# Attention values divided in their transposed layout after small transfers, and the context tiles transposed beside the value tiles

## The reference, cut to what matters

```python
# x: (8, 512, 256); ctx: (8, 1601, 256); 16 heads of 16; 704 hidden
def attention(query, ctx):                       # per batch
    q, k, v = split_heads(query @ Wq.T + bq), split_heads(ctx @ Wk.T + bk), split_heads(ctx @ Wv.T + bv)
    attn = softmax(einsum('bhqd,bhkd->bhqk', q, k) / 4)
    out = einsum('bhqk,bhkd->bhqd', attn, v)     # merged heads: (512, 256)
    return out @ Wo.T + bo
x = x + attention(layernorm(x), ctx)
h = layernorm(x)                                 # fp4_linear rounds both operands
h = silu(fp4_linear(h, w_gate)) * fp4_linear(h, w_up)
x = x + fp4_linear(h, w_down)                    # to a 4-bit grid in blocks of 16
```

## Time and profile before

| | before |
|---|---|
| median of 3 runs | 1804.52 us (1801.16 to 1804.56) |
| the profiled execution: time, span | 1801.16 us, 1799.4 us |
| mean granted clock of TensorE | 0.984 |
| TensorE busy | 1687.2 us (94%) |
| VectorE busy | 1398.6 us (78%) |
| ScalarE busy | 1155.4 us (64%) |
| GpSimd busy | 528.4 us (29%) |
| loop iteration | about 210 us |

### The profile page before, as it was taken

The page is one execution under the profiler, slowest core; times in us unless marked ns, Lnnn a source line. Parts: engine busy times, 40 slices in busy tenths (PEclk is TensorE's granted clock), DMA queues, the critical chain, the costliest instruction groups (busy, mean ns, idle before and its releaser), DMA issues.

```text
span 1799.4 us, 26659 instructions
## 1 busy us (share of the span) xinstructions
PE 1687.2 (94%) x9600; PEld 658.4 (37%) x9600; DVE 1398.6 (78%) x1969; ACT 1155.4 (64%) x2335; POOL 528.4 (29%) x409
## 2 busy tenths in 40 slices
PE   3799789999999999999999999999999999989978
PEld 2332124333343343433443333433334334423425
DVE  6777887888868887788878888688877887688538
ACT  2366567776667666776667766676667766666651
POOL 4316340442107320152204421073201622012213
PEclk8899999999999999999999999999999999999989
DMA  6643432142323322043221423243220422300000
GB/s 147 151 77 92 90 77 37 47 116 38 55 37 96 91 49 50 13 110 73 55 52 44 118 40 55 37 96 90 50 48 12 108 40 43 52 1 1 7 18 12
DMA packets 98031, 109.09 MB, mean 61 GB/s; under 512 B 18788, under 2 KB 83308, under 8 KB 97900
## 3 DMA queue, kind: packets, MB, share of 16 engines
q1 hardware_dynamic: 93344, 103.26, 27.1%
q10 hardware_dynamic: 4556, 4.13, 1.1%
HBM read 76.78 MB, written 30.16 MB: 59 GB/s over the span
## 4 chain that ended last, share of the span: by engine, by line
PE 74%; DVE 15%; ACT 7%; issue 3%; DMA 1%; ACTq 0%; POOL 0%; SPq 0%; DVEq 0%; POOLq 0%
PE pvb L714 19%; PE st L685 18%; PE mx L699 9%; PE misc L632 7%; DVE cmx L941 6%; PE misc L582 5%; ACT prob L870 4%; PE misc L589 4%; PE misc L644 2%; PE misc L652 2%; PE misc L521 1%; PE misc L640 1%; PE misc L611 1%; PE misc L570 1%; PE misc L559 1%
## 5 line engine op out<-in xcount | busy, mean ns | idle before, releaser
L870 ACT ACTIVATE prob<-st 128x512 f32<-128x512 f32 x1630 | 887.6, 599 | 419.9 <-PE st L685 418.2
L941 DVE TENSOR_REDUCE cmx<-mx 128x2 f32<-128x1024 f32 x768 | 905.3, 1219 | 215.4 <-PE mx L699 211.7
L685 PE MATMUL st<-qstack,kstack 112*128 112x512 bf16 x1630 | 520.6, 386 | 32.6 <-ACT prob L870 20.0
L714 PE MATMUL pvb<-prob,vv 128*17 128x512 f32 (+1 forms) x3328 | 440.7, 601 | 0.6 <-ACT prob L870 0.6
L685 PEld LDWEIGHTS st<-qstack,kstack 112*128 112x128 bf16 x1630 | 128.4, 98 | 554.9 <-issue 315.7
L699 PE MATMUL mx<-kstack,qstack 48*128 48x512 bf16 (+1 forms) x2048 | 253.3, 336 | 32.8 <-DMA qstack<-scr_q 16.3
L1202 POOL TENSOR_TENSOR cin<-cin 128x400 f32<-128x400 f32 (+1 forms) x60 | 55.3, 922 | 418.6 <-ACT cin L798 418.6
L1235 POOL TENSOR_TENSOR ht<-ht,rh 128x704 f32<-128x704 f32 x29 | 40.2, 1385 | 425.0 <-DVE rh L917 425.0
L632 PE MATMUL misc<-wguT,rowsT 128*128 128x352 f32 x456 | 154.9, 462 | 0.0
L699 PEld LDWEIGHTS mx<-kstack,qstack 48*128 48x128 bf16 x2048 | 58.0, 94 | 195.7 <-issue 147.2
L632 PEld LDWEIGHTS misc<-wguT,rowsT 128*128 128x128 f32 x456 | 87.1, 191 | 41.4 <-issue 1.0
(11 more groups left out here) (201 smaller groups left out, 1593.3 us busy)
## 6 DMA issues: line engine op xcount, KB each, us to landing
kstack<-scr_k SPq DMA_DIRECT2D x384, 100.1 KB, 4.3
scr_k<-cin SPq DMA_DIRECT2D x48, 300.0 KB, 3.2
qstack<-scr_q SPq DMA_DIRECT2D x372, 32.0 KB, 1.9
cin<-ctx_in SPq DMA_DIRECT2D x8, 1280.0 KB, 6.6
scr_q<-qp SPq DMA_DIRECT2D x15, 384.0 KB, 5.4
scr_k<-cin SPq DMA_DIRECT2D x16, 300.8 KB, 4.4
xn<-x SPq DMA_DIRECT2D x8, 512.0 KB, 3.9
x<-x SPq DMA_DIRECT2D x8, 512.0 KB, 3.8
```

The lines of the kernel that those rows point to most:

```text
L685: mm(score_bank(it, n, pair, h)[0:KROWS[kt], :], kstack[:, hd, KOFF[kt]:KOFF[kt] + KROWS[kt]], qstack[:, hd, :], start=True, stop=True).th ...
L714: last = mm(pvb[32 * h:32 * h + D + 1, :], vv[0:w, kt, HG * g + h, :], prob[0:w, n % 2, h, :], start=(kt == 0), stop=(kt == NKT - 1))
L870: activate(prob[0:KROWS[kt], n % 2, 2 * pair + h, :], score_bank(it, n, pair, h)[0:KROWS[kt], :], ACT.Exp, scale=SCALE).then_inc(exp_done[ ...
L941: v.tensor_reduce(cmx[:, g % 2, h0:h0 + 2, at:at + 1], products, op=ALU.max, axis=AX.X).then_inc(max_free, 1)
```

## The change

- `vv` holds, for each pair of heads, 16 values, 16 ones, 16 values. A head's weights are 32 columns (values and ones, or ones and values), so `pvb` has for each head 16 rows of weighted values and 16 rows that all hold the sum of weights.
- `pvT`, `attT`, `den`, `attTr` and `group_divided` go. After the copy to `pvs`, SP moves for each group four pieces of 16 rows by 512 to `att`, whose layout is now the transposed one, and four to `sums` (`values_in`; in the tail ScalarE's queue takes the four of `sums`). When two groups are there, VectorE takes the reciprocal of `sums` in place (512 columns) and multiplies `att` in place (`values_divided`), in steps 37 and 3. `o` reads `att`.
- Context tiles are transposed one by one, as a `guest` of the value tile of the same number: the two transposes go into the free half of its bank, behind its matmuls. ScalarE copies them behind the values. `ctx2`, two tiles at once, is left for the start.
- `q` 0, `q` 1 and the keys stand in other steps, and GpSimd's work follows: in step 16 `xround` now comes first, then the split of `k` 4.
- `nm` 1 is in step 9; `bias` waits for value tile 9; `xnT` shares its memory with `mt`, so `xpower` waits for `q` 1.
- SP's order: the values' transfers come in, and the keys of one half are stored together.

```diff
 SLOTS = {
-    0: ([("v", 8, "att")], [("ctxT", 0, "early")]),
-    1: ([("v", 9, "att")], [("pvT", 3, "late")]),
-    2: ([("v", 10, "att")], [("attT", 0, "late")]),
-    3: ([("v", 11, "att")], [("attT", 1, "late")]),
-    4: ([("v", 12, "att")], [("ctxT", 1, "early")]),
-    5: ([("o", 0, "late")], [("ctxT", 2, "early")]),
-    6: ([("o", 1, "late")], [("ctxT", 3, "early")]),
-    7: ([("ctxT", 4, "early")], [("ctxT", 5, "early")]),
-    8: ([("ctxT", 6, "early")], [("xnT", 0, "early")]),
-    9: ([("k", 0, "early")], [("xnT", 1, "early")]),
-    10: ([("k", 1, "early")], [("nm", 1, "att")]),
-    11: ([("k", 2, "early")], []),
-    12: ([("q", 0, "early")], []),
+    0: ([("v", 8, "att")], [("ctx2", 0, "once")]),
+    1: ([("v", 9, "att")], [("ctx2", 1, "once")]),
+    2: ([("v", 10, "att")], [("ctx2", 2, "once")]),
+    3: ([("v", 11, "att")], [("ctx2", 3, "once")]),
+    4: ([("v", 12, "att")], []),
+    5: ([("o", 0, "late")], []),
+    6: ([("o", 1, "late")], []),
+    7: ([("xnT", 0, "early")], []),
+    8: ([("xnT", 1, "early")], []),
+    9: ([("q", 0, "early")], [("nm", 1, "att")]),
+    10: ([("k", 0, "early")], []),
+    11: ([("k", 1, "early")], []),
+    12: ([("k", 2, "early")], []),
     13: ([("k", 3, "early")], []),
-    14: ([("k", 4, "early")], []),
-    15: ([("q", 1, "early")], []),
+    14: ([("q", 1, "early")], []),
+    15: ([("k", 4, "early")], []),
     16: ([("k", 5, "early")], []),
     17: ([("k", 6, "early")], []),
-    18: ([("pvT", 0, "att")], [("xqT", 0, "late")]),
-    19: ([("k", 7, "early")], [("xqT", 1, "late")]),
+    18: ([("xqT", 0, "late")], [("xqT", 1, "late")]),
+    19: ([("k", 7, "early")], []),
...
-    31: ([("gate", 5, "late")], [("pvT", 1, "att")]),
+    31: ([("gate", 5, "late")], []),
...
-    41: ([("down", 2, "late")], [("pvT", 2, "att")]),
+    41: ([("down", 2, "late")], []),
...
 DVE_EXTRA = {
-    1: [("late", "norm", 3)], 5: [("late", "stats", 0)], 6: [("late", "stats", 1)], 7: [("late", "mean", 0)], 8: [("late", "root", 0)],
-    9: [("late", "apply", 0)], 10: [("att", "nm", 1)], 11: [("late", "apply", 1)], 12: [("late", "xmax", 0)], 13: [("late", "xscale", 0)],
-    14: [("late", "xmul", 0)], 15: [("late", "xpower", 0)], 17: [("late", "xlast", 0)], 19: [("att", "norm", 0)],
+    3: [("late", "values", 1)], 5: [("late", "stats", 0)], 6: [("late", "stats", 1)], 7: [("late", "mean", 0)], 8: [("late", "root", 0)],
+    9: [("att", "nm", 1)], 10: [("late", "apply", 0)], 11: [("late", "apply", 1)], 12: [("late", "xmax", 0)], 13: [("late", "xscale", 0)],
+    14: [("late", "xmul", 0)], 15: [("late", "xpower", 0)], 17: [("late", "xlast", 0)],
...
-    31: [("att", "norm", 1)], 33: [("late", "hscale", 2)], 34: [("late", "hpower", 2)], 35: [("att", "nm", 3)], 39: [("late", "hscale", 3)], 40: [("late", "hpower", 3)],
-    42: [("att", "norm", 2)], 43: [("next", "stats", 0)], 44: [("next", "stats", 1)], 45: [("next", "mean", 0)], 46: [("next", "root", 0)],
+    33: [("late", "hscale", 2)], 34: [("late", "hpower", 2)], 35: [("att", "nm", 3)], 37: [("att", "values", 0)], 39: [("late", "hscale", 3)], 40: [("late", "hpower", 3)],
+    43: [("next", "stats", 0)], 44: [("next", "stats", 1)], 45: [("next", "mean", 0)], 46: [("next", "root", 0)],
...
 POOL_WORK = {
-    0: [("late", "bias", 0)], 10: [("early", "k", 0)], 11: [("early", "k", 1)], 12: [("early", "k", 2)], 13: [("early", "q", 0)],
-    14: [("early", "k", 3)], 15: [("early", "k", 4)], 16: [("early", "q", 1), ("late", "xround", 0)], 17: [("early", "k", 5)], 18: [("early", "k", 6)], 20: [("early", "k", 7)],
+    0: [("late", "bias", 0)], 10: [("early", "q", 0)], 11: [("early", "k", 0)], 12: [("early", "k", 1)], 13: [("early", "k", 2)],
+    14: [("early", "k", 3)], 15: [("early", "q", 1)], 16: [("late", "xround", 0), ("early", "k", 4)], 17: [("early", "k", 5)], 18: [("early", "k", 6)], 20: [("early", "k", 7)],
...
+            def values_in(it, g, part):
+
+                sp.wait_ge(pvs_done, it.count(part, NG, g + 1))
...
+                for h in range(HG):
+                    row = HALF * s + D * h
+                    values, weights = 2 * D * h + D * (h % 2), 2 * D * h + D * (1 - h % 2)
+                    sp.dma_start(att[row:row + D, c, :], pvs[values:values + D, :]).then_inc(values_row[g], 16)
+                    if it.kind != "tail":
+                        sp.dma_start(sums[row:row + D, :], pvs[weights:weights + D, :]).then_inc(values_row[g], 16)
...
                     last.then_inc(full[kind], 1)
+                    if guest(it, job):
+                        context_tile(guest(it, job))
...
-                        last = mm(pvb[32 * h:32 * h + D + 1, :], vv[0:w, kt, HG * g + h, :], prob[0:w, n % 2, h, :], start=(kt == 0), stop=(kt == NKT - 1))
+                        last = mm(pvb[2 * D * h:2 * D * (h + 1), :], vv[0:w, kt, (HG * g + h) // 2, D * (h % 2):D * (h % 2 + 2)], prob[0:w, n % 2, h, :], start=(kt == 0), stop=(kt == NKT - 1))
...
+                def values_divided(part, c):
+
+                    for g in (2 * c, 2 * c + 1):
+                        dve.wait_ge(values_row[g], it.count(part, 128, 128))
+                    v.reciprocal(sums[:, :], sums[:, :]).then_inc(rec_ready, 1)
+                    dve.wait_ge(rec_ready, it.count(part, NC2, c + 1))
+                    v.tensor_tensor(att[:, c, :], att[:, c, :], sums[:, :], ALU.mult).then_inc(att_ready, 1)
...
                         pool.wait_ge(s_x1, c(16, 16))
+                        if it.kind != "tail":
+
+                            pool.wait_ge(free["v"], it.count("att", NKT, 10))
```

More of the change, by code:

```diff
@@ L123 @@
 PRE_SLOTS = {
-    5: ([("ctxT", j, "early") for j in range(7)], []),
+    5: ([("ctx2", j, "early") for j in range(7)], []),
     8: ([("xnT", j, "early") for j in range(2)], []),
@@ L333, in job_count, with tiles_turned, guest @@
         def job_count(it, job):
-            return it.count(job[2], PER[job[0]], job[1] + 1)
+            kind, j, part = job
+            if kind == "ctx2":
+                return (PAIRS if part == "once" else 0) + j + 1
+            if part == "once":
+                return j + 1
+            if kind == "ctxT":
+                return tiles_turned(it, part, j + 1)
+            return it.count(part, PER[kind], j + 1)
+        def tiles_turned(it, part, k):
+            return (it.batch(part) - 2) * NKT + NKT - 8 + k
+        def guest(it, job):
+            if job[0] != "v" or it.kind == "pre":
+                return None
+            part = {"early": "next", "att": "early"}[job[2]]
+            return ("ctxT", job[1], part) if part in it.parts else None
         def job_bank(it, job):
+            if job[0] == "ctxT":
+                return misc[:, 2 * 128:]
             b = BANKS.bank(it.kind, job)
@@ L472, in body @@
                     return
+                if has_late:
+                    values_in(it, 3, "late")
                 if has_att:
@@ L663, in shared, with context_tile @@
                     last.then_inc(full[kind], 1)
+                    if guest(it, job):
+                        context_tile(guest(it, job))
+                def context_tile(job):
+                    _, j, part = job
+                    if j in (0, 2, NKT - 1) or j == 8 and it.kind == "first":
+                        pe.wait_ge(s_ctx[0 if j == 0 else 2 if j == NKT - 1 else 1], it.count(part, 16, 16))
+                    w, o = KROWS[j], job_bank(it, job)
+                    for h in range(NC2):
+                        last = turn(o[:, h * 128:h * 128 + w], ctx_rows[0:w, j, h * 128:(h + 1) * 128], ident[0:w, 0:w])
+                    last.then_inc(full["ctxT"], 1)
                 def scores(n, pair):
@@ L849, in take @@
                         raw_in(j // 2 + 2)
+                    if guest(it, job):
+                        take(guest(it, job))
                 def first_queries():
@@ L873, in group_out @@
                     act.wait_ge(pv_done, it.count(part, STEPS, NKT * (g + 1)))
-                    if g:
-                        act.wait_ge(full["pvT"], it.count(part, NG, g))
+                    need(act, values_row[(g - 1) % NG], it.count(part, 128, 128 if g else 0))
                     copy(pvs[:, :], pvb[:, :]).then_inc(pvs_done, 1)
+                    if it.kind == "tail":
+                        act.wait_ge(pvs_done, it.count(part, NG, NG))
+                        for h in range(HG):
+                            row, weights = HALF + D * h, 2 * D * h + D * (1 - h % 2)
+                            act.dma_start(sums[row:row + D, :], pvs[weights:weights + D, :]).then_inc(values_row[g], 16)
                 has_att, has_late = "att" in it.parts, "late" in it.parts
```

119 lines of the change are left out of this document (64 added, 55 removed).

## The result

The changed kernel takes 1839.01 us (median of 4 runs, 1838.14 to 1841.43) against 1803.67 us for the kernel before (4 runs, 1801.16 to 1804.56): a ratio of 1.020, 95% interval 1.0183 to 1.0218. That is 2% slower. The forecast was 1850 us, with a range from 1806 to 1874.

The account below looks back on a forecast made before the run. TensorE's order of work was taken to set the pace, with a late VectorE able to stop it. Loop +39.3, first iteration +3.5, last +2, tail +4.3: +49 on 1801.2 gives 1850 us, range 1806 to 1874.

Parts of the forecast that it names:

- The key split waits: Steps 17 and 18: ScalarE's evacuation of `k` 6 waits for GpSimd's late split of `k` 4, +6.4 us per loop iteration.
- The clock: TensorE's clock at half after stalls: 2.0 us behind the 6.4 us stall, 1.0 behind the 2.7 us one, per loop iteration.
- The divisions: VectorE's 512-wide reciprocals, 3.4 us each, stall step 5 by 1.45 us and step 38 by 2.7 us per loop iteration.
- Removed work: Each loop iteration: transposes gone or joined to `v`, `q` and key jobs in new places, bias moved; -7.0 us in all.
- Wider weights: The `pvb` matmuls in every step: 32 weight columns for 17 cost nothing, since they still stream 512 columns; 0 us.
- The transfers: SP queue: eight more per group, 5.3 us, delay nothing outside the tail; 0 us, 1 to 4 per batch if uncovered.
- The first iteration: First iteration: the same trades without `o` and `xround`, about 0, plus the stall near step 38 with its clock, +3.5 us.
- The last iteration: Last iteration: -3.3 us from five transpose groups, against +1.65, +2.7 (stall) and +1.0 (clock); +2 us.
- The tail: End of the kernel: copy of `pvs`, uncovered transfers and a 4.1 us division; +4.3 us.
- The rival of the free key split: Step 17: `k` 4's split ends before ScalarE needs the buffer, no wait; 1783 to 1800 us, middle 1792; chance 0.13.
- The rival of covered divisions: Steps 5 and 38: a `values` under 1.3 us fits VectorE's slack, no stalls; 1808 us; chance 0.05 alone.

## Why the prediction was right, step by step

The side, the cause and the order of the stalls were right. The sum was 11 us too high, and some of its terms came out by luck.

- **The key split waits** (+6.4 forecast). Shown from both sides. `k` 6 was ready at 793.75 and evacuated at 799.11: 5.4 us. TensorE's scores came 5.1 us late by it; the forecast had not parted ScalarE's delay from TensorE's. The rounding and the split took what the earlier trace rows had (the split ends 3.68 us behind the rounding, 3.66 before), but the rounding stood 1.05 us earlier against `k` 6 than before, where the forecast had let `xpower` only move along with step 15. `xpower`'s two operations took 1.07 and 1.53 us before, while GpSimd split `q` 1, and 0.68 and 0.69 now, while GpSimd stood still. This is read from the traces and was not tried by itself, but other rows bear it out. In the last iteration of the kernel before, which splits no `q` 1, the two operations also take 0.68 and 0.69 us. In the kernel before with the late split, where `q` 1 is split beside them again, they take 1.07 and 1.53, and the delay is the 6.4 us of the forecast.
- **A wait that the forecast lacked.** Under the key split's wait lay the one of `xqT` 0 for `xlast`. So freeing the key split won only 3.9 of the 7.1 us that steps 18 and 19 had lost. The forecast's sum holds because the two waits lie over each other, and that is luck: it gave the whole stretch to the key split.
- **The clock** (+3.0). Steps 18 and 19 lost 7.1 us (14.99 less the 7.90 planned, which no run took). TensorE's wait is 5.1 of them, which leaves an estimated 2.0 for the clock, as forecast. Steps 38 and 39 lost 4.04, of which 2.3 are TensorE's wait: 1.7 for the clock, where 1.0 was forecast. Together 3.7. Here the clock fell behind the short stall in all six iterations; in the kernel with the split first it did so in four of six, and each time it cost 1.6 us (11.8 for 10.16). The forecast's "sometimes" is right in kind, and how often is chance as far as these runs show.
- **The divisions.** The reciprocal takes 3.34 us, where the slope of the earlier trace rows gave 3.4; 128 columns take 0.943, on the same line. The Trainium skill (VectorE: DVE Perf Modes, "First, the fixed hardware budget") names a repeat count of 8, and the forecast's estimate from it was 4.3 us. The trace doesn't agree with that estimate, and the measurement decides: 3.34 us for 512 elements, 6.5 ns each. The stalls were 1.15 us (1.45 forecast) and 2.3 to 2.4 us (2.7).
- **Removed work** (-7.0). Steps 0 to 4 gave 0.45 more than forecast: a `v` with its guest is 3.53 to 3.59 us, not 3.66, and step 4, whose tile has 65 rows instead of 128, is at the floor with 3.49. In steps 42 to 51 the guest costs 0.09 to 0.14 us, not 0.19. Both say that more of the first side is hidden in the floor than the line through `up` and `o` gave. Steps 9 to 20 without 18 and 19 take 40.09 us; 39.9 was forecast. Step 49 got shorter by 0.75 (0.67 forecast), a good half of it by the bias.
- **Wider weights** (0 forecast, +3 to 4 us measured in the whole kernel). The eight matmuls stream the same columns, but their loads are longer, and this is not all hidden.
- **The transfers** on SP (0 forecast). The seventeen steps that the change doesn't touch are 0.25 us longer together, no more than the weights explain, and the 2.4 us of a landing show nowhere but in the tail.
- **The first iteration** came out 3.8 us lower than forecast. Its stall is there (steps 39 to 41 are 3.6 us longer), but the rest, forecast at about 0, became shorter by 3.9, 1.8 of them in step 33.
- **The last iteration** came out 0.9 lower, and that close only by luck. The stall at step 38 is 0.4 us there instead of 2.7 with 1.0 for the clock. `xqT` 0 on the first side waits 1.9 us for `xlast`, which the forecast lacked, and makes steps 18 and 19 2.5 us longer.
- **The tail** came out 2.0 higher: 0.6 by slower transfers, and the rest lies behind them, where `o` runs at half clock.
- **The start.** The 4.1 us ahead of the first `pvb` group were not forecast. A part is a longer stretch at half clock there (from 45.0 to 48.4 us the granted clock is 0.50, and 0.96 before). With the same code ahead of it this group came at 88.2 to 90.5 us in the kernels built on the changed one, and at 86.2 to 86.3 in the kernel before and the two built on it, so 2 to 4 us are the change's; which part of it does that stays open.

Against the forecast's +49: the loop -13.6, the first and last iterations -4.7, the tail +2.0, the start +4.1, together 12 less, and +37 was measured on the span.

- **The rival of the free key split** (1783 to 1800, middle 1792) was wrong in its price as well as in its condition. With the split made free the kernel takes 1813, because `xqT` 0 on the first side of step 18 waits for `xlast`. The forecast had it at 4.06 us with "`xqT` twice, the first hidden", and did not ask when its rows are ready. Only the kernel with that undone too, at 1800.73, comes to the edge of that rival's range.
- **The rival of covered divisions** fell with the 3.34 us. With a copy in the reciprocal's place its condition was met, and the kernel took 1794 us, 14 less than its price; the saving itself was 45 us for 42 forecast, so most of the 14 are what the whole sum was too high by. As for the piece under 1.3 us that it named as fitting into a step's slack: it does fit, as the kernel with four pieces shows.

Where the gain went is thus accounted for: of the 1839 us, taken away in this order, 26 are the split behind the rounding, 12 `xqT` 0 on the first side, and 26 the first division in one piece. Without the three the changed kernel takes 1774.96 us, 28.5 less than the kernel before. The second division at step 5, the longer tail and the later start are still in that.

## What to carry to other kernels

When work moves between tables of several engines, write down for each moved item when its input is ready and who waits behind it, on the engines with idle time too: a queue that is 29% busy cost 26 us by the order of two entries. An operation on an engine that serves every step must be shorter than one step's slack there, or be cut until it is; its total hardly matters. And when one long wait is taken away, look for the shorter one that it hid.

## What the runs showed of the hardware

- Behind a wait of TensorE of 2.2 to 2.3 us the granted clock may go to half for 3.4 us or stay. With TensorE busy 1.07 and 1.08 of 3.40 us, it was at half behind the one and at 1.00 behind the other. A fall cost 1.6 us of steps beyond the wait. Behind the wait of 5.06 us it fell each time, and steps 18 and 19 took 14.0 to 15.5 us.
- In these traces VectorE and GpSimd slow each other on operations in SBUF. VectorE's conversions of 128x1024 took 1.07 and 1.53 us beside GpSimd's split and 0.68 and 0.69 alone; GpSimd's third split operation took 1.81 us beside a multiply of VectorE and 0.89 to 0.96 where VectorE did not; a cast of 16x128 took 2.18 us beside the bias and 0.20 alone.
- A reciprocal of 44, 64, 128 and 512 columns took 0.428, 0.553, 0.943 and 3.34 us, so 6.1 to 6.3 ns for each further column and some 0.15 us besides. A plain copy of 512 columns took 0.42 us.
- Transfers of 16 partitions by 2 KB within SBUF took a median of 0.59 us to issue and 2.4 us to land, against 0.42 and 1.9 in the earlier trace rows.
- 32 columns of fp32 weights load in 108 to 109 ns, 17 in 95 ns, and 3 to 4 us of that came through over 3328 such loads.
